# Transformer block with routed experts on one NeuronCore: attention keys and queries in two parts of 11 bits instead of three parts of 8, and one score product for two heads instead of two

## The chip, the cores and the metric

The kernel runs on one core of one Trainium2 chip. The core has a matrix engine (TensorE, PE in the profile; its weight loads are PEld), VectorE (DVE), ScalarE (ACT) and GpSimd (POOL), and SyncE (SP) that issues most DMAs. Each engine runs its own instructions in order; they meet through semaphores. The metric is the device time of one execution in microseconds.

## What is computed

Input z is (4, 1024, 256) in float32. The part that this change touches is the attention of 16 heads of 16 dimensions:

```python
x = L0_attn_z
zn = layernorm(layernorm(x)) * ln_scale + ln_bias
q, k, v = split(zn @ w_qkv)            # 16 heads of 16
scores = einsum('bhqd,bhkd->bhqk', q, k) / 4
att = softmax(scores)                  # over 1024 keys
out = einsum('bhal,bhlv->bhav', att, v) @ w_proj + b_proj
x = x + layernorm(layernorm(x) + out)
# then a gated feed-forward with 8 routed experts (top 1) for every second token,
# x = x + layernorm(ffn(layernorm(x)))
```

## The kernel before

The four batches run through one pipeline of **slots**. A batch has 64 slots: 4 groups of 4 heads, two halves of 512 queries, 8 tiles of 128 keys (`SL = 64`, 256 slots for all). Slot t does the **max products** of slot t and the **scores** of the slot 12 earlier (`LEAD = 12`).

*Scores.* A float32 score is made of 16-bit products. A key or query is split in three bfloat16 parts of 8 bits; `PRODUCTS` lists six pairs of parts that are kept. The six times 16 dimensions do not fit in the 64 rows that one head has of the 128, so they stand in two planes: plane 0 has the pairs of the largest parts (48 rows), plane 1 the other three and two rows with the negated maximum (50 rows). `kp` and `qp` hold them, stacked by DMAs (`STACK`, `pack_step`, L377 to L396). Two heads, one in rows 0 to 63 and one in rows 64 to 127, run at the same time. `scores(a)` (a = 0 and 1, two heads each) issues four matmuls of 512 columns: two planes, two heads (L1047). ScalarE takes the exp of the 1024 columns (L870) and `value_product` multiplies them with the values in float32 (L1061).

*Maxima.* The softmax needs each query's largest score before. It is taken from plane 0 alone: four max products a slot (L1028), each into one bank of the PSUM **ring** of three banks, each reduced by VectorE (L1324). Every 8 slots the maxima are transposed ("mt"), split in two parts (`mp`, L1332 and L1334) and sent by DMA into the last two rows of `qp`.

*The ring* also takes all other results: transposes of normalized inputs ("z", "x", "u"), projections of keys and queries ("qk"), values ("v"), the output ("p") and the feed-forward ("h", "w"). `ring_order` writes by hand in which slot each stands (`Z_AT`, `QK_AT` and so on); in a slot they come before max0. Bank i is free again when the engine that takes the item three places earlier is done.

*On TensorE* a slot has: ring items of other kinds, max products 0 and 1, `scores(0)`, `scores(1)`, max products 2 and 3, and the value products of the slot before.

*The parts.* ScalarE copies a projection to `qkf` (L805) and its first part to `parts` (L807). Then three passes over 1024 columns: the residual (`residual`, L1314 on VectorE or L640 on GpSimd), the second part as its cast (L646, or L1377 at the start) and the third part (L649, L1379). For the next batch's first keys VectorE makes the residual in slot 35 and GpSimd the other two.

Of the kernel before, what the change touches and what calls it, by code (L numbers as in the profile page):

```python
# [14 lines left out]
GH = 4  # L15
# [6 lines left out]
KM = KR + 2  # L22
# [6 lines left out]
PRODUCTS = [(0, 0), (1, 0), (0, 1), (2, 0), (1, 1), (0, 2)]  # L29
STACK = [(par, r // 3 * 4, 64 * par + r % 3 * HD, k, q) for r, (k, q) in enumerate(PRODUCTS) for par in range(2)]  # L30
# [103 lines left out]
def plane_of(h, plane):  # L134

    return h // 8 * 8 + 4 * plane + h % 8 // 2


def build(nc, x, ln_params, w_q, w_k, w_v, w_proj, b_proj, index_b, index_t, sw12, sb12, sw3, sb3,
          hidden_ln, gate_w, gate_b, exp_bias, ew12, ebias12, ew3, eb3, out):  # L140
    f32, bf16, i32, u32 = mybir.dt.float32, mybir.dt.bfloat16, mybir.dt.int32, mybir.dt.uint32
# [9 lines left out]
    with ExitStack() as ctx:  # L151
# [19 lines left out]
        parts = sb("parts", [P, 2, 3, N], bf16)  # L171
        qp = sb("qp", [P, NH, H, HALF], bf16)
        kp = sb("kp", [P, H, N], bf16)
# [25 lines left out]
        mp = sb("mp", [GH * QT, 2, 2, P], bf16)  # L199
# [42 lines left out]
        fixed = resid[0:2, 0:HALF].bitcast(bf16)  # L242
# [38 lines left out]
        s_resid = sem("residual_of_first_part")  # L281
        s_second = sem("second_part")
        s_third = sem("third_part")
# [78 lines left out]
        LARGEST = [item for item in STACK if item[1] == 0]  # L362
        REST = [item for item in STACK if item[1] > 0]
# [11 lines left out]
        def _(sp):  # L375
# [3 lines left out]
            def pack_step(b, c, i):  # L379


                for n in range(3 * i, 3 * i + 3):
                    if n in (0, len(STACK)):
                        sp.wait_ge(s_third, 2 * KD * b + c + (n > 0) + 1)
                        if b > 0:
                            sp.wait_ge(s_av, SL * (b - 1) + (SL // 2 if c < 2 else SL))
                    par, plane, row, k, q = STACK[n if n < len(STACK) else (n - len(STACK)) // NH]
                    rows, h0, src = slice(row, row + HD), c // 2 * 8 + plane, slice(par * 64, par * 64 + 64)
# [42 lines left out]
            for par in range(2):  # L431
                for h in (0, 8):
                    first = plane_of(h, 1)
                    sp.dma_start(kp[64 * par + KR:64 * par + KM, first:first + 4, :],
# [6 lines left out]
            for part in range(2):  # L441
                if part == 1:
                    sp.wait_ge(s_second, 1)
                for par, plane, row, k, q in LARGEST:
                    if k == part:
                        sp.dma_start(kp[row:row + HD, plane:plane + 4, :], parts[par * 64:par * 64 + 64, 0, k, :])\
                          .then_inc(s_k0, 16)
            sp.wait_ge(s_part, 4)
            for part in range(2):
                if part == 1:  # L450
                    sp.wait_ge(s_second, 2)
                for par, plane, row, k, q in LARGEST:
                    if par == 1 and q == part:
                        sp.dma_start(qp[row:row + HD, 0, plane:plane + 4, :],
# [1192 lines left out]
```

## Time and profile before

| what | value |
|---|---|
| median of 3 runs | 995.28 us (992.9 to 995.99) |
| profiled execution | 993.8 us, its span 992.0 us |
| TensorE busy | 927.3 us (93%) |
| VectorE busy | 798.6 us (81%) |
| ScalarE busy | 617.0 us (62%) |
| GpSimd busy | 352.1 us (35%) |
| score products, L1047, 2048 of them | 275.2 us |
| max products, L1028, 1024 | 246.4 us |
| value products, L1061, 2048 instructions | 273.6 us |

Times of rows are microseconds from the start of the span. In a timeline a row is: start, length, engine, line, operation, out<-in, shapes, how many were merged, and in brackets the idle time before it with what ended it. The rows of the windows view have: from and to, its length, busy time and number of instructions of PE, PEld, DVE, ACT and POOL, then the granted clock of TensorE as a share of its full speed, the DMA share and GB/s. "L1028 <- DVE mx L1324" in a wait says that VectorE's instruction of line 1324 ended it. A float32 matmul is two instructions. A matmul's row lasts from its start until its last column is written, and the next one starts before that.

### The profile page before, as it was taken

What the parts mean: (1) busy time and instruction counts of PE and PEld (TensorE: products, weight loads), DVE (VectorE), ACT (ScalarE), POOL (GpSimd) and SP (SyncE); (2) the same over time, 40 slices, a digit from 0 to 9 for tenths busy, and PEclk for the clock granted to TensorE, in tenths of its full rate; (3) what the DMA queues carried; (4) which work ended last, traced back from release to release, by engine and by line L of the source; (5) the groups of instructions that cost most, each with busy time, mean ns of one, the idle gap of its engine ahead of it and who ended that gap; (6) DMA issues with size and microseconds to landing.
All of it is one profiled execution on the core that took longest, in us unless ns stands there. A gap on an engine that the chain in (4) does not pass through costs nothing.

```text
span 992.0 us, 16504 instructions
## 1 busy us (share of the span) xinstructions
PE 927.3 (93%) x6202; PEld 373.5 (38%) x6204; DVE 798.6 (81%) x1568; ACT 617.0 (62%) x720; POOL 352.1 (35%) x473
## 2 busy tenths in 40 slices
PE   5879999999999999999999999999999989957985
PEld 3323332323343344333343343332422423136763
DVE  4688879898979878889889979889799798265765
ACT  3116778777867777777767767777676777801110
POOL 3052003004635253229733623258243232822113
PEclk9778999999999999999999999999999999988998
DMA  4924120620260305300631033104430000240001
GB/s 135 155 32 64 47 55 12 98 61 8 75 109 24 97 13 77 75 13 22 113 110 60 8 54 80 36 8 104 91 99 13 12 13 20 95 170 22 1 0 64
DMA packets 60544, 58.14 MB, mean 59 GB/s; under 512 B 19136, under 2 KB 49680, under 8 KB 60080
## 3 DMA queue, kind: packets, MB, share of 16 engines
q1 hardware_dynamic: 59840, 55.83, 25.6%
q8 instruction: 49, 0.80, 0.4%
q0 software_dynamic: 384, 1.05, 0.3%
q10 hardware_dynamic: 240, 0.20, 0.2%
q14 instruction: 31, 0.25, 0.1%
HBM read 18.06 MB, written 9.17 MB: 27 GB/s over the span
## 4 chain that ended last, share of the span: by engine, by line
PE 79%; DVE 9%; ACT 3%; issue 3%; DMA 2%; POOL 2%; SPq 1%; ACTq 0%; POOLq 0%; DVEq 0%
PE obank L1061 22%; PE sc L1047 19%; PE ring L1028 16%; PE ring L946 9%; PE ring L953 4%; DVE mx L1324 4%; PE sc L1178 3%; PE ring L938 2%; DVE st L1253 2%; ACT prob L870 1%; PE sc L953 1%; DMA x_sb<-x 1%; DMA qp<-parts 1%; PE ring L1071 1%; ACT zT L773 0%
## 5 line engine op out<-in xcount | busy, mean ns | idle before, releaser
L1324 DVE TENSOR_REDUCE mx<-ring 128x1 f32<-128x512 f32 x1024 | 634.6, 681 | 107.9 <-PE ring L1028 106.9
L870 ACT ACTIVATE prob<-sc 128x1024 f32<-128x1024 f32 x512 | 495.8, 1021 | 132.6 <-PE sc L1047 131.4
L1047 PE MATMUL sc<-qp,kp 48*128 48x512 bf16 (+1 forms) x2048 | 275.2, 380 | 2.2 <-DMA qp<-mp 0.9
L1061 PE MATMUL obank<-prob,vaug 128*32 128x512 f32 x2048 | 273.6, 606 | 0.7 <-ACT prob L870 0.7
L1028 PE MATMUL ring<-kp,qp 48*128 48x512 bf16 x1024 | 246.4, 392 | 17.0 <-DVE mx L1324 13.0
L1028 PEld LDWEIGHTS ring<-kp,qp 48*128 48x128 bf16 x1024 | 75.0, 93 | 296.4 <-DVE mx L1324 228.5
L1047 PEld LDWEIGHTS sc<-qp,kp 48*128 48x128 bf16 (+1 forms) x2048 | 98.9, 95 | 106.8 <-ACT prob L870 25.2
L626 POOL TENSOR_TENSOR hid<-hid,b 128x512 f32<-128x512 f32 x24 | 30.3, 1271 | 110.9 <-ACT hid L831 110.9
L1061 PEld LDWEIGHTS obank<-prob,vaug 128*32 128x32 f32 x2048 | 40.3, 108 | 66.1 <-issue 63.9
L640 POOL TENSOR_TENSOR resid<-qkf,parts 128x1024 f32<-128x1024 f32 x11 | 23.4, 2131 | 114.4 <-ACT parts L807 114.4
L634 POOL TENSOR_TENSOR yA<-yA,sums 128x512 f32<-128x512 f32 x15 | 19.0, 1269 | 110.4 <-DMA sums<-reciprocal_scratch 110.4
L646 POOL TENSOR_SCALAR parts<-resid 128x1024 bf16<-128x1024 f32 x14 | 14.7, 1050 | 106.7 <-DVE resid L1314 105.7
L946 PE MATMUL ring<-w,yT 128*128 128x256 f32 x192 | 47.6, 400 | 1.4 <-ACT yT L773 1.4
L946 PEld LDWEIGHTS ring<-w,yT 128*128 128x128 f32 x192 | 36.7, 198 | 16.8 <-DVE mx L1324 5.0
L938 PE MATMUL ring<-ident,zn 128*128 128x128 f32 x128 | 19.4, 303 | 23.9 <-DVE zn L1351 12.1
L805 ACT ACTIVATE qkf<-ring 128x512 f32<-128x512 f32 x28 | 16.7, 595 | 30.5 <-PE ring L953 29.1
L572 POOL TENSOR_TENSOR sum_m<-st 128x8 f32<-128x8 f32 x15 | 3.1, 209 | 79.6 <-DVE st L1253 79.6
L649 POOL TENSOR_TENSOR parts<-resid,parts 128x1024 bf16<-128x1024 f32 x14 | 29.8, 2131 | 1.2
L773 ACT ACTIVATE yT<-ring 128x512 f32<-128x512 f32 x16 | 8.8, 595 | 33.2 <-PE ring L938 33.2
L1178 PE MATMUL sc<-kp,qp 128*128 128x256 f32 x128 | 29.1, 381 | 0.1
L946 PE MATMUL ring<-wv,zT 128*128 128x256 f32 x128 | 28.8, 379 | 0.0
L938 PEld LDWEIGHTS ring<-ident,zn 128*128 128x128 f32 x128 | 16.4, 157 | 28.6 <-issue 12.9
(212 smaller groups left out, 797.9 us busy)
## 6 DMA issues: line engine op xcount, KB each, us to landing
kp<-parts SPq DMA_DIRECT2D x96, 128.0 KB, 4.9
qp<-parts SPq DMA_DIRECT2D x189, 64.0 KB, 2.9
x_sb<-x SPq DMA_DIRECT2D x7, 1024.0 KB, 6.1
out<-hid SPq DMA_DIRECT2D x4, 1024.0 KB, 5.3
yA<-oT SPq DMA_DIRECT2D x124, 32.0 KB
sums<-reciprocal_scratch SPq DMA_DIRECT2D x31, 128.0 KB
x_scratch<-x SPq DMA_DIRECT2D x3, 1024.0 KB, 4.5
qp<-mp SPq DMA_DIRECT2D x128, 2.0 KB
```

Source lines behind the costliest of these rows:

```text
L626: nc.gpsimd.tensor_tensor(hid[:, t, :], hid[:, t, :], {"h": b12, "w": b3}[kind][:, :] .rearrange("p (o d) -> p o d", o=1).to_broadcast([P, ...
L640: nc.gpsimd.tensor_tensor(resid[:, :], qkf[:, :], parts[:, c % 2, 0, :], ALU.subtract)\
L649: nc.gpsimd.tensor_tensor(parts[:, c % 2, 2, :], resid[:, :], parts[:, c % 2, 1, :], ALU.subtract).then_inc(s_third, 1)
L870: nc.scalar.activation(prob[:, e % 2, 2 * a:2 * a + 2, :].rearrange("p g n -> p (g n)"), sbuf2[a][:, :], ACT.Exp, scale=0.25).then_inc(s_f ...
L938: ins = nc.tensor.transpose(dst[:, t * P:(t + 1) * P], src[:, 4 * h + t, kk * P:(kk + 1) * P], ident[:, :])
L946: ins = nc.tensor.matmul(dst[:, (t - 2 * i) * D:(t - 2 * i + 1) * D], src[:, k, t * P:(t + 1) * P], w[:, k, :], start=(k == 0), stop=(k == ...
L953: ins = nc.tensor.matmul(dst[:, :], w[:, k, mt * P:(mt + 1) * P], zT[:, k, h * HALF:(h + 1) * HALF], start=(k == 0), stop=(k == KD - 1))
L1028: nc.tensor.matmul(dst[:, :], qp[rows, qh, h, qt * P:(qt + 1) * P], kp[rows, h, kh * HALF:(kh + 1) * HALF], start=True, stop=True).then_in ...
L1047: ins = nc.tensor.matmul(dst[:, j * HALF:(j + 1) * HALF], kp[rows, h, kt * P:(kt + 1) * P], qp[rows, qh, h, :], start=plane == 0, stop=pla ...
L1061: ins = nc.tensor.matmul(obank[i * VW:(i + 1) * VW, :], vaug[:, b % 2, kt, c0:c0 + VW], prob[:, v % 2, i, :], start=(kt == 0), stop=(kt == ...
L1178: ins = nc.tensor.matmul(expert_bank(i)[:, t, :], lhs[:, m], w, start=False, stop=stop, skip_group_check=True)
L1324: nc.vector.tensor_reduce(mx[:, u % 2, n:n + 1], src[:, :], AX.X, ALU.max).then_inc(rv_free, 1)
```

## The change

Keys and queries are scaled by a power of two each, so that they fit in float16, and split in two float16 parts of 11 bits. Four pairs of parts are kept, the smallest of them in 14 of the 16 dimensions: 3 x 16 + 14 + 2 rows for the maximum are the 64 rows of a head. So one matmul makes a head's scores. The max products are the same first 48 rows.

```diff
-KM = KR + 2
+KS = HD - 2
+KM = KR + KS + 2
-PRODUCTS = [(0, 0), (1, 0), (0, 1), (2, 0), (1, 1), (0, 2)]
+PRODUCTS = [(0, 0), (1, 0), (0, 1), (1, 1)]
...
-                    for plane in range(2):
-                        h = plane_of(g * GH + 2 * a, plane)
-                        for j in range(2):
-                            rows = slice(64 * j, 64 * j + (KM if plane else KR))
-                            ins = nc.tensor.matmul(dst[:, j * HALF:(j + 1) * HALF], kp[rows, h, kt * P:(kt + 1) * P],
-                                                   qp[rows, qh, h, :], start=plane == 0, stop=plane == 1)
+                    h = g * GH // 2 + a
+                    for j in range(2):
+                        rows = slice(64 * j, 64 * j + KM)
+                        ins = nc.tensor.matmul(dst[:, j * HALF:(j + 1) * HALF], kp[rows, h, kt * P:(kt + 1) * P],
+                                               qp[rows, qh, h, :], start=True, stop=True)
```

A part now takes one pass in place of three, on VectorE for the first two parts of the kernel and on GpSimd for all others; the one of slot 35 moves from VectorE to GpSimd, slot 34:

```diff
-            def split(b, c):
-                n = 2 * KD * b + c
-                pool.wait_ge(s_resid, n + 1)
-                nc.gpsimd.tensor_scalar(parts[:, c % 2, 1, :], resid[:, :], 1.0, 0.0, ALU.mult, ALU.add)\
                     .then_inc(s_second, 1)
-                pool.wait_ge(s_second, n + 1)
-                nc.gpsimd.tensor_tensor(parts[:, c % 2, 2, :], resid[:, :], parts[:, c % 2, 1, :],
-                                        ALU.subtract).then_inc(s_third, 1)
...
-                if w + 1 < B and tau == 35:
-                    split(w + 1, 0)
+                if w + 1 < B and tau == 34:
+                    second_part(w + 1, 0)
```

The scales come from a bound made at the start: the weights times the layer norm's scale and bias are squared on ScalarE, summed over their rows by a matmul with ones, the largest taken on VectorE, its root on GpSimd, and a power of two of it on VectorE. ScalarE applies the scale as it evacuates a projection, and the exp takes it out again; both scales are operands in memory, one per partition:

```diff
+            for a, w in enumerate((wk, wq)):
+                for k in range(KD):
+                    for r in range(2):
+                        nc.scalar.activation(wsq[:, a, k, r, :], w[:, k, :], ACT.Square, scale=lnp[:, r, k:k + 1])\
+                            .then_inc(s_wsq, 1)
...
-                    nc.scalar.activation(qkf[:, half], src[:, :], ACT.Copy).then_inc(taken, 1)
+                    nc.scalar.activation(qkf[:, half], src[:, :], ACT.Identity, scale=scale[:, c % 2:c % 2 + 1]).then_inc(taken, 1)
...
-                                             sbuf2[a][:, :], ACT.Exp, scale=0.25).then_inc(s_free, 1)
+                                             sbuf2[a][:, :], ACT.Exp, scale=unscale[:, 0:1]).then_inc(s_free, 1)
...
-                for n in range(3 * i, 3 * i + 3):
+                for n in range(2 * i, 2 * i + 2):
...
-                    nc.vector.tensor_copy(mp[:, u % 2, 0, :], src[0:GH * QT, 0:P]).then_inc(s_m1, 1)
+                    nc.vector.tensor_scalar(mp[:, u % 2, 0, :], src[0:GH * QT, 0:P], 1.0 / MAX_ROW, None, ALU.mult)\
+                        .then_inc(s_m1, 1)
...
-                    nc.vector.tensor_tensor(mp[:, u % 2, 1, :], src[0:GH * QT, 0:P], mp[:, u % 2, 0, :],
-                                            ALU.subtract).then_inc(rv_free, 1)
-
-            nc.vector.memset(fixed[:, :], 1.0).then_inc(s_src, 1)
+                    nc.vector.scalar_tensor_tensor(mp[:, u % 2, 1, :], src[0:GH * QT, 0:P], 1.0 / MAX_ROW,
+                                                   mp[:, u % 2, 0, :], ALU.mult, ALU.subtract).then_inc(rv_free, 1)
```

TensorE's instructions of a slot, before. `ring0` to `ring2` are the ring's banks, `sc0` and `sc1` the two score banks; L1071 is the maxima's transpose, so this is a slot with one of them:

```order
L1071 MATMUL ring0<-ident,nm 16x128 [waits negated_maxima,ring_taken_by_vector]
L1028 MATMUL ring1<-kp,qp 128x512 [waits ring_taken_by_vector]
L1028 MATMUL ring2<-kp,qp 128x512 [waits ring_taken_by_vector]
L1047 MATMUL sc0<-qp,kp 128x512 [waits score_buffer_taken]
L1047 MATMUL sc0<-qp,kp 128x512 x3
L1047 MATMUL sc1<-qp,kp 128x512 [waits score_buffer_taken]
L1047 MATMUL sc1<-qp,kp 128x512 x3
L1028 MATMUL ring0<-kp,qp 128x512 [waits ring_taken_by_vector]
L1028 MATMUL ring1<-kp,qp 128x512 [waits ring_taken_by_vector]
L1061 MATMUL obank<-prob,vaug 32x512 [waits score_buffer_taken]
L1061 MATMUL obank<-prob,vaug 32x512 x3
```

The same slot with the change:

```order
L1080 MATMUL ring0<-ident,nm 16x128 [waits negated_maxima,ring_taken_by_vector]
L1038 MATMUL ring1<-kp,qp 128x512 [waits ring_taken_by_vector]
L1038 MATMUL ring2<-kp,qp 128x512 [waits ring_taken_by_vector]
L1056 MATMUL sc0<-qp,kp 128x512 [waits score_buffer_taken]
L1056 MATMUL sc0<-qp,kp 128x512
L1056 MATMUL sc1<-qp,kp 128x512 [waits score_buffer_taken]
L1056 MATMUL sc1<-qp,kp 128x512
L1038 MATMUL ring0<-kp,qp 128x512 [waits ring_taken_by_vector]
L1038 MATMUL ring1<-kp,qp 128x512 [waits ring_taken_by_vector]
L1070 MATMUL obank<-prob,vaug 32x512 [waits score_buffer_taken]
L1070 MATMUL obank<-prob,vaug 32x512 x3
```

Four score products are gone; nothing else moved, and the fourth max product still goes to the bank of the first, `ring1`.

ScalarE's first instructions, before (`zT` is the transposed input, `lnp` the layer norm's scale and bias):

```order
L839 ACT_TABLE_LOAD
L839 ACTIVATE ex<-mhalf 128x2 [waits exponents_made]
L773 ACTIVATE zT<-ring,lnp 128x512 [waits ring_filled,attention_weights_loaded]
L773 ACTIVATE zT<-ring,lnp 128x512 [waits ring_filled] x3
L805 ACTIVATE qkf<-ring 128x512 [waits ring_filled]
L807 ACTIVATE parts<-qkf 128x512 [waits ring_taken_by_scalar]
```

And with the change (`hid` and `act` are buffers that are free at the start):

```order
L835 ACT_TABLE_LOAD
L835 ACTIVATE ex<-mhalf 128x2 [waits exponents_made]
L840 ACTIVATE hid<-wk,lnp 128x256 [waits attention_weights_loaded]
L840 ACTIVATE hid<-wk,lnp 128x256 x3
L840 ACTIVATE hid<-wq,lnp 128x256 x4
L768 ACTIVATE zT<-ring,lnp 128x512 [waits ring_filled] x4
L801 ACTIVATE qkf<-ring,scale 128x512 [waits scales_of_keys_and_queries,ring_filled]
L803 ACTIVATE parts<-qkf 128x512 [waits ring_taken_by_scalar]
```

Eight squares stand before the first evacuation, and TensorE has eight small matmuls that wait for them before its first transpose.

## Rows read from the trace of the kernel before

**Rows 1.** The page's chain that ended last, by line.
```profile
PE obank L1061 22%; PE sc L1047 19%; PE ring L1028 16%; PE ring L946 9%; PE ring L953 4%; DVE mx L1324 4%; PE sc L1178 3%; PE ring L938 2%; DVE st L1253 2%; ACT prob L870 1%; PE sc L953 1%; DMA x_sb<-x 1%; DMA qp<-parts 1%; PE ring L1071 1%; ACT zT L773 0%
```
**Rows 2.** Busy time by windows: first slots with scores, and a stretch of the middle.
```profile
72.60:84.20 11.60, 11.24 (x53) 3.32 (x52) 8.33 (x14) 5.45 (x6) 8.21 (x14) 0.57 0.95 108
...
100.00:300.00 200.00, 199.48 (x1452) 69.68 (x1451) 174.49 (x311) 150.04 (x171) 48.00 (x51) 1.00 0.28 58
```
**Rows 3.** Waits from 100 to 840 us: total, times, longest.
```profile
PEld ring L1028 <- DVE mx L1324: 197.3, 384, 3.2
```
**Rows 4.** Timeline of TensorE in one plain slot, 262.13 to 264.62.
```profile
262.13 0.39 PE L1028 MATMUL ring<-kp,qp 48*128 48x512 bf16 x2
...
262.36 1.03 PE L1047 MATMUL sc<-qp,kp 48*128 48x512 bf16 x8
...
263.23 0.46 PE L1028 MATMUL ring<-kp,qp 48*128 48x512 bf16 x2
263.30 0.09 PEld L1028 LDWEIGHTS ring<-kp,qp 48*128 48x128 bf16 x1 [0.19 <-DVE mx L1324]
...
263.62 1.06 PE L1061 MATMUL obank<-prob,vaug 128*32 128x512 f32 x8
...
264.62 0.39 PE L1028 MATMUL ring<-kp,qp 48*128 48x512 bf16 x2
```
**Rows 5.** Timeline of a slot after two transposes of z.
```profile
256.41 1.45 ACT L773 ACTIVATE zT<-ring,lnp 128x512 f32<-128x512 f32 x2 [0.55 <-PE ring L938]
...
256.68 0.39 PE L1028 MATMUL ring<-kp,qp 48*128 48x512 bf16 x1
...
257.24 0.39 PE L1028 MATMUL ring<-kp,qp 48*128 48x512 bf16 x1 [0.17 <-ACT zT L773]
...
258.65 1.07 PE L1061 MATMUL obank<-prob,vaug 128*32 128x512 f32 x8
```
**Rows 6.** Timeline of a slot after two transposes of x, TensorE.
```profile
358.87 0.70 PE L1028 MATMUL ring<-kp,qp 48*128 48x512 bf16 x2
...
360.59 1.06 PE L1061 MATMUL obank<-prob,vaug 128*32 128x512 f32 x8
```
**Rows 7.** Timeline of the slot after the next batch's second projection, TensorE.
```profile
345.09 0.60 PE L1047 MATMUL sc<-qp,kp 48*128 48x512 bf16 x4
...
345.96 0.61 PE L1047 MATMUL sc<-qp,kp 48*128 48x512 bf16 x4 [0.27 <-ACT prob L870]
```
**Rows 8.** Timelines of the last twelve slots, without max products: ScalarE and TensorE.
```profile
852.11 1.05 PE L1047 MATMUL sc<-qp,kp 48*128 48x512 bf16 x8 [0.91 <-DMA qp<-mp]
...
862.26 1.02 ACT L870 ACTIVATE prob<-sc 128x1024 f32<-128x1024 f32 x1
...
863.61 3.91 ACT L870 ACTIVATE prob<-sc 128x1024 f32<-128x1024 f32 x4 [0.33 <-PE sc L1047]
867.85 1.94 ACT L870 ACTIVATE prob<-sc 128x1024 f32<-128x1024 f32 x2 [0.33 <-PE sc L1047]
```
**Rows 9.** ScalarE's groups by shape: count, busy us, mean ns of one, idle.
```profile
L773 ACT ACTIVATE zT<-ring,lnp 128x512 f32<-128x512 f32 x16 | 11.8, 774 | 14.0 <-PE ring L938 13.8
...
L773 ACT ACTIVATE yT<-ring 128x512 f32<-128x512 f32 x16 | 8.8, 595 | 33.2 <-PE ring L938 33.2
...
L909 ACT ACTIVATE zT<-ring,hln 128x256 f32<-128x256 f32 x2 | 1.1, 562 | 1.7 <-PE ring L1199 1.7
...
L904 ACT ACTIVATE zn<-sc 128x256 f32<-128x256 f32 x2 | 0.8, 383 | 16.2 <-PE sc L1178 16.2
```
**Rows 10.** Timeline of the start.
```profile
3.29 0.47 SPq L429 DMA_DIRECT2D wv<-w_v  x1
...
12.13 3.65 PE L938 MATMUL ring<-ident,zn 128*128 128x128 f32 x16 [12.13 <-DVE zn L1351]
...
22.92 0.69 DVE L1377 CAST parts<-resid 128x1024 bf16<-128x1024 f32 x1
```
**Rows 11.** DMA issues of the first 40 us: KB each, us to landing.
```profile
wv<-w_v SPq DMA_DIRECT2D x1, 256.0 KB, 5.3
```

More of the change, by code:

```diff
@@ L25 @@
 MT = M // P
-PRODUCTS = [(0, 0), (1, 0), (0, 1), (2, 0), (1, 1), (0, 2)]
-STACK = [(par, r // 3 * 4, 64 * par + r % 3 * HD, k, q) for r, (k, q) in enumerate(PRODUCTS) for par in range(2)]
+PRODUCTS = [(0, 0), (1, 0), (0, 1), (1, 1)]
+STACK = [(par, HD if r < 3 else KS, 64 * par + r * HD, k, q) for r, (k, q) in enumerate(PRODUCTS) for par in range(2)]
+TOP = 2.0 ** 13
+MAX_ROW = 2.0 ** 15
 ONES = struct.unpack("<f", struct.pack("<HH", 0x3F80, 0x3F80))[0]
@@ L198, in build @@
         nm = sb("nm", [P, 2, GH * QT])
-        mp = sb("mp", [GH * QT, 2, 2, P], bf16)
+        mp = sb("mp", [GH * QT, 2, 2, P], f16)
+        wmax, wroot, power, scale, unscale = (sb(n, [P, 2]) for n in ("wmax", "wroot", "power", "scale", "unscale"))
         st6 = [sb(f"st6{i}", [P, NT, 6]) for i in range(2)]
@@ L663, in _ @@
             rstd_of("z", 0, 0, NT, 0)
+            pool.wait_ge(s_wmax, 1)
+            step(nc.gpsimd.tensor_scalar(wroot[:, :], wmax[:, :], 2.0 * D, 1e-30, ALU.mult, ALU.add))
+            nc.gpsimd.tensor_tensor(wroot[:, :], wroot[:, :], mhalf[:, 0:2], ALU.pow).then_inc(s_wroot, 1)
             pool.wait_ge(s_rstd["z"], 1)
@@ L670, in _ @@
                 if tau == (4 if w == 0 else 3) and w < B:
-                    residual(w, 2)
-                    split(w, 2)
+                    second_part(w, 2)
                 if tau == (11 if w == 0 else 4) and w + 1 < B:
@@ L675, in _ @@
                 if tau == (6 if w == 0 else 5) and w < B:
-                    residual(w, 3)
-                    split(w, 3)
+                    second_part(w, 3)
                 if w == B - 1 and tau == 5:
@@ L713, in _ @@
                 if w + 1 < B and tau == 40:
-                    residual(w + 1, 1)
-                    split(w + 1, 1)
+                    second_part(w + 1, 1)
                 if 1 <= w < B:
@@ L866, in _ @@
                     if 0 <= e < NS:
+                        if e == 0 and a == 0:
+                            sc.wait_ge(s_power, 4)
                         if e >= 2 and a == 0:
@@ L1003, in _ @@
             pe.wait_ge(s_first, C_FIRST)
+            pe.wait_ge(s_ones, 1)
+            for a in range(2):
+                for i in range(2 * KD):
+                    pe.wait_ge(s_wsq, 2 * KD * a + i + 1)
+                    ins = nc.tensor.matmul(sbuf2[0][:, a * D:(a + 1) * D], ones, wsq[:, a, i // 2, i % 2, :], start=(i == 0),
+                                           stop=(i == 2 * KD - 1))
+                ins.then_inc(s_bound, 1)
             for key in RING_AT[-1]:
@@ L1355, in _ @@
             ins.then_inc(s_norm["z"], 1)
+            ve.wait_ge(s_bound, 2)
+            nc.vector.tensor_reduce(wmax[:, :], sbuf2[0][:, 0:2 * D].rearrange("p (a d) -> p a d", a=2), AX.X, ALU.max)\
+                .then_inc(s_wmax, 1)
             ve.wait_ge(s_idxin, 32)
@@ L1423, in _ @@
                     nc.vector.tensor_tensor(half, half, sums[0:GH * HD, 1, :], ALU.mult).then_inc(s_div64, 1)
-                if w + 1 < B and tau == 35:
-                    residual(w + 1, 0)
                 if 1 <= w < B and tau in (47, 49):
```

113 lines of the change are left out of this document (59 added, 54 removed).

## Prediction

> **What bounds the kernel now.** The page first. Its chain puts 19% of the span on the score products (L1047) [rows 1], and in the middle of the kernel TensorE shows matmuls for 199.48 of 200 us, VectorE 174.49 [rows 2]. Read so far, the score products are the thing to halve. But each matmul's row lasts longer than the step to the next one, so short waits lie hidden under it. The list of waits shows them: weight loads of the max products (L1028) waited 197.3 us for VectorE's reductions between 100 and 840 us, 384 times [rows 3].
>
> So one plain slot has to be read instruction by instruction [rows 4]. Its four max products go to the three ring banks; call them max0 to max3. Max3 gets the bank that max0 had, and so waits until VectorE has reduced max0. In the slot that starts at 262.13:
> - max0 and max1 at 262.13, eight score products from 262.36, max2 at 263.23;
> - the weights of max3 at 263.30, after a wait that VectorE ended: 1.17 after max0;
> - the value products at 263.62 (0.32 later), the next max0 at 264.62 (1.00 later).
>
> 1.17 + 0.32 + 1.00 is the slot's 2.49 us, and this loop (max0, its reduction, max3, value products, next max0) does not contain the score products. They fill time that TensorE would wait through, with 0.07 us to spare (263.23 against 263.30). Projections and transposes stand between the value products and the next max0, so their time adds to the loop and is paid in full before and after the change. By my count of the slots from 12 to 255, nine in ten have this form.
>
> A rule of the Trainium skill fits what this row shows (Trainium Kernel Development and Optimization, Performance Expectations): matmul busy time is a bad measure of distance to the roofline, because matmuls are pipelined. The chain's share, read as time to be won, would give 100 us or more; rows 4 give nothing in such a slot.
>
> **The change part by part.** The sum is made against the profiled execution, 993.8 us, which is 1.5 under the median of 995.28.
>
> *Four score products in place of eight, plain slots.* Two pairs go, 0.44 us of the 0.87 between 262.36 and 263.23. Max2 is issued 0.44 earlier, max3 still at +1.17. Gain 0 [rows 4].
>
> *Slots in which max3 is late for another reason.* Where a transposed z or u is evacuated, max1 waits for ScalarE and pushes the score products back, and max3 comes after them [rows 5]: max1 goes at 257.24, the value products at 258.65. With four score products TensorE is through them by 257.9; max2 needs the second evacuation (256.41 + 1.45 = 257.86), max3 the reduction of max0 (256.68 + 1.17 = 257.85). The value products come at about 258.24: 0.41 won. There are six z slots and three of u alike: 3.7 us. In the six x slots the value products start 1.72 after max0 instead of 1.49 [rows 6]: 0.23 each, 1.4 us. In batches 1 and 2 one slot has its second half of scores 0.87 after the first instead of 0.44, waiting for an exp [rows 7]; the exp is late because ScalarE waited for VectorE's residual, which GpSimd, idle there, now makes a slot earlier. 0.43 less the spare 0.07 is 0.35, twice: 0.7 us. Eight slots with a shortfall of 0.03 add 0.2. Together 6.0 (5.0 to 6.2, the lower end if the exp stays late).
>
> *The first slots with scores.* The granted clock is 0.57 there [rows 2], mostly the lower level, and TensorE, not VectorE, sets the pace. The two pairs cost 0.86 at that level: 0.86 in two slots and about half in the third, 2.2 in all. But if the clock comes back at the same time as before, the work that arrives 1.7 us sooner finds it low for longer, and some 1.0 is given back. I take 1.2, bounds 0 and 2.2.
>
> *The twelve slots after the last max product.* Only scores, exps and value products run. Two slots take 4.24 us (863.61 to 867.85), of which ScalarE works 3.91 and waits 0.33 for scores [rows 8]. With short score products ScalarE is the bound. Its exps get a scale from memory. The price of that is bounded by evacuations: with scale and bias from memory 774 ns against 595 at 512 columns, 562 against 383 at 256, so 179 for both together whatever the length [rows 9]. I take half, 0.09, for the scale alone; bounds 0 and 0.18. Two exps back to back take 1.94 and one alone 1.02 [rows 8], so 0.92 from start to start; four take 4 x 1.01 = 4.04, 0.10 won a slot. Two of the slots end in a wait of 0.91 for the maxima's rows [rows 8] that swallows it: ten slots, 1.0 us (at 0.18: 4.40, a loss of 0.8).
>
> The Trainium skill (ScalarE: Activation LUTs, What ACT_TABLE_LOAD costs) gives about 93 ns for each pointer operand, so it splits the pair's 179 ns evenly. By it the sum is the same; with all 179 on the scale it is the rival below.
>
> *Exps in the other slots.* 0.09 on two exps is met by scores that are ready 0.22 sooner, and two exps fit in 2.49 with 0.5 to spare. 0.
>
> *The start.* New before the first transposes: eight squares on ScalarE and eight small matmuls. The last weights were issued at 3.29 and took 5.3, so they are there at 8.6 to 9.1 [rows 10, 11]. A 128x256 evacuation takes 383 [rows 9]; with one pointer and an overlap of 0.1, some 0.38 a square, 3.0 us: done at 11.7 to 12.2. The small matmuls follow each square, so the transposes start at 12.0 to 12.5 instead of 12.13 [rows 10]: 0.2 lost (0 to 0.4). The root and the powers of two run on GpSimd and VectorE while TensorE transposes and projects. Against that, a part's 0.69 us cast [rows 10] leaves the way between the second query part and its DMA, on which the first max product waits. ScalarE's two pointer evacuations there take 0.2 of it back. Net 0.3 won (0.4 lost to 0.7 won).
>
> *Hidden, at 0.* A residual on VectorE (three times, under the projection of keys and queries); two of three GpSimd passes for each part; a third of the stacking DMAs and their issues on SP (no TensorE wait for them stands in the middle); two small ops in the maxima's split, of the same size as those replaced. A slot with its transpose that ran longer by 0.1 would cost 3 us over 32.
>
> *Sum.* 6.0 + 1.2 + 1.0 + 0.3 = 8.5. 993.8 - 8.5 = 985.3; at the median's level 995.28 - 8.5 = **986.8 us**. Bounds of the terms: 3.8 to 10.1, so 985.2 to 991.5; with the 1.5 us by which runs of the kernel before scatter, 983.5 to 993.
>
> **The rivals.**
> *The score products are on the path*, as the chain says [rows 1]. Then 244 slots win 0.44 each: 107 us, 888. Against it: max3's wait is ended by VectorE [rows 3, 4].
>
> *The clock falls in the middle (slower).* TensorE will wait longer in each plain slot. It had the lower level for most of 72.6 to 84.2, a stretch in which it waited, and 1.00 between 100 and 300 [rows 2], with 0.19 of waiting in a plain slot [rows 4]. At the lower level the value products take 2.0 instead of 1.0, so a slot is at least 3.5. A low stretch of 11.6 us, as that one, then holds 3.3 slots instead of 4.7 and costs 3.4. From three such stretches on nothing is won; if half of the middle were low it would cost 100. At six of them, 8.5 - 6 x 3.4 = -11.9, it is 1,007.
> The Trainium skill has the rule behind it (TensorE: Matmul & The Clock Gate, Part 1): the clock is gated by how busy the engine has been, and low is the resting state. No row shows a plain slot with half its score products.
>
> *The start gives it back.* With other work at the start the low stretch that ends near 84 us [rows 2] lasts longer, or another one is added: one or two times 3.4 us, 990 to 994.
>
> *The scale pointer costs 0.18 an exp.* The last slots lose 0.8 instead of winning 1.0, and in some 14 slots after keys and queries the exps run late by up to 0.2: 8.5 - 1.8 - 2.5 = 4.2, 991.1.
>
> *It does not do what it says.* The order has half the score instructions, so only their rate can fail: no row has the 16-bit float type of the change. The nearest is the other 16-bit type, 0.22 a pair [rows 4], and I take that. At twice that time two more pairs stand in the loop of each slot, 0.44 x 244: 1,095 us.
>
> **How the numbers follow.** Forecast 0.64; scores on the path 0.03; clock in the middle 0.08; start gives it back 0.12, nearly half of it under 992.3; scale pointer 0.10; 16-bit rate 0.03. The band of 0.3%, about what a measurement of this kernel can tell, is 992.3 to 998.3. Faster: 0.64 + 0.03 + 0.10 + 0.05 = 0.82; same 0.08; slower 0.10, the clock, the rate and little else. The range 981 to 993.5 takes in the forecast, the scale pointer and the better half of the start.
>
> **What would show it.** In the profile after: plain slots still 2.49 from max0 to max0, the wait of max3's weights grown from 0.19 to about 0.6 and ended by VectorE; TensorE's busy time down by tens of microseconds with the span down by under ten; z slots with value products 1.56 after max0, x slots 1.49; exps at 1.11 instead of 1.02; the last slots at 2.0; the first transposes by 12.5. I am wrong if plain slots get shorter, if the clock between 100 and 840 us is under 1.00, or if exps grow by 0.18.

## The result and the profile after

| | before | after |
|---|---|---|
| median | 994.89 us (4 runs, 992.9 to 995.99) | 984.22 us (4 runs, 983.47 to 986.59) |
| profiled execution, its span | 993.8, 992.0 us | 983.9, 982.1 us |
| TensorE busy | 927.3 us | 882.3 us |
| ScalarE busy | 617.0 us | 663.7 us |
| score products | 275.2 us, 2048 of them | 167.9 us, 1024 of them |

The ratio after to before is 0.9899, 95% interval 0.9876 to 0.9923: 10.7 us by the medians, 9.9 by the two profiled executions. The forecast was 986.8, within 981 to 993.5.

The groups of the page (line, engine, operation, out<-in, shapes, count | busy us, mean ns | idle before and what ended it) and the wait that answers to [rows 3]:

```profile
L873 ACT ACTIVATE prob<-sc,unscale 128x1024 f32<-128x1024 f32 x512 | 539.1, 1113 | 85.2 <-PE sc L1056 83.9
L1038 PEld LDWEIGHTS ring<-kp,qp 48*128 48x128 f16 x1024 | 74.1, 93 | 361.4 <-DVE mx L1331 301.3
L1056 PE MATMUL sc<-qp,kp 64*128 64x512 f16 x1024 | 167.9, 381 | 14.0 <-ACT prob L873 13.3
L801 ACT ACTIVATE qkf<-ring,scale 128x512 f32<-128x512 f32 x28 | 19.2, 686 | 27.1 <-PE ring L956 25.7
```
```profile
PEld ring L1038 <- DVE mx L1331: 267.1, 393, 3.4
```

The rows of the score products lost 107 us, TensorE as a whole 45 (rows of matmuls overlap, and those of the max products are drawn longer now: 299.4 us for 246.4). The max products' weights wait 70 us more for VectorE (197.3 to 267.1, between 100 and 840 us before, 90 and 830 after). So most of the time saved became waiting.

The plain slot of [rows 4] is now this one:

```profile
262.73 0.39 PE L1038 MATMUL ring<-kp,qp 48*128 48x512 f16 x2
...
262.95 0.60 PE L1056 MATMUL sc<-qp,kp 64*128 64x512 f16 x4
...
263.39 0.90 PE L1038 MATMUL ring<-kp,qp 48*128 48x512 f16 x2
...
263.89 0.09 PEld L1038 LDWEIGHTS ring<-kp,qp 48*128 48x128 f16 x1 [0.60 <-DVE mx L1331]
...
264.21 1.06 PE L1070 MATMUL obank<-prob,vaug 128*32 128x512 f32 x8
...
265.21 0.39 PE L1038 MATMUL ring<-kp,qp 48*128 48x512 f16 x2
```

Max2 comes 0.66 us after max0 instead of 1.10, and still max3's weights come after 1.16 and the next max0 after 2.48. The wait grew from 0.19 to 0.60.

**Where the time went**, slot by slot (start of max0 to start of the next, both traces; gains positive):

| stretch | gain, us |
|---|---|
| until slot 12 begins (72.7 to 69.2) | 3.5 |
| slots 12 to 14, the first with scores | 2.4 |
| six z and three u slots, 0.42 each | 3.7 |
| six x slots, 0.23 each | 1.4 |
| slots 100 and 164, behind keys and queries, 0.28 each | 0.6 |
| slots 79, 143, 207 and 212 | 1.9 |
| ten slots with 0.05 more each | -0.5 |
| slots 218, 241 and 242, at the lower clock | -3.6 |
| the last twelve slots | 1.3 |
| behind them | -0.7 |

These add up to 10.0, for 9.9 measured. A z slot and an x slot of after, beside [rows 5, 6]:

```profile
250.23 0.39 PE L1038 MATMUL ring<-kp,qp 48*128 48x512 f16 x1
...
251.78 1.07 PE L1070 MATMUL obank<-prob,vaug 128*32 128x512 f32 x8
252.78 0.39 PE L1038 MATMUL ring<-kp,qp 48*128 48x512 f16 x2
```
```profile
354.46 0.71 PE L1038 MATMUL ring<-kp,qp 48*128 48x512 f16 x2
...
355.95 1.07 PE L1070 MATMUL obank<-prob,vaug 128*32 128x512 f32 x8
```

The value products start 1.55 (z) and 1.49 us (x) after max0; the prediction had 1.56 and 1.49. The stretches at the lower clock, as windows (times, length, busy of PE, PEld, DVE, ACT, POOL, granted clock, DMA share, GB/s), and the wait ahead of the second:

```profile
714.10:717.50 3.40, 3.40 (x16) 0.60 (x13) 3.04 (x6) 2.12 (x2) 3.21 (x5) 0.50 0.05 5
789.20:796.00 6.80, 6.50 (x27) 1.17 (x29) 4.61 (x8) 2.12 (x2) 6.26 (x17) 0.50 0.06 22
```
```profile
789.50 0.60 PE L1038 MATMUL ring<-kp,qp 48*128 48x512 f16 x1 [3.08 <-DVE mx L1331]
```

Between 100 and 300 us the clock is 1.00 as before.

The stretch at the lower clock into which the first slots with scores fall, before, after, and in the experiment "Score products alone" below:

```profile
62.10:82.60 20.50, 17.11 (x54) 4.37 (x55) 17.52 (x35) 3.88 (x4) 13.84 (x26) 0.50 0.68 87
```
```profile
58.70:75.80 17.10, 14.06 (x37) 2.69 (x37) 16.49 (x33) 4.24 (x4) 8.63 (x21) 0.50 0.50 68
```
```profile
59.20:79.60 20.40, 17.22 (x55) 4.39 (x57) 17.42 (x34) 4.45 (x5) 10.45 (x24) 0.50 0.42 57
```

### The profile page after: what moved, and what is told of

Read it like the earlier page. It is cut to its first block and busy times, and to the rows that moved or that the text cites. A ratio compares the mean times of both kernels' runs of the same rounds, so it can differ in the third digit from the quotient of the medians.

```text
span 982.1 us, 14337 instructions
## 1 busy us (share of the span) xinstructions
PE 882.3 (90%) x5188; PEld 319.8 (33%) x5188; DVE 792.7 (81%) x1568; ACT 663.7 (68%) x728; POOL 314.5 (32%) x450
## 3 DMA queue, kind: packets, MB, share of 16 engines
q0 software_dynamic: 384, 1.05, 0.3%
## 5 line engine op out<-in xcount | busy, mean ns | idle before, releaser
L873 ACT ACTIVATE prob<-sc,unscale 128x1024 f32<-128x1024 f32 x512 | 539.1, 1113 | 85.2 <-PE sc L1056 83.9
L1038 PE MATMUL ring<-kp,qp 48*128 48x512 f16 x1024 | 299.4, 395 | 43.5 <-DVE mx L1331 22.5
L1038 PEld LDWEIGHTS ring<-kp,qp 48*128 48x128 f16 x1024 | 74.1, 93 | 361.4 <-DVE mx L1331 301.3
L1056 PE MATMUL sc<-qp,kp 64*128 64x512 f16 x1024 | 167.9, 381 | 14.0 <-ACT prob L873 13.3
L644 POOL TENSOR_TENSOR parts<-qkf,parts 128x1024 f16<-128x1024 f32 x14 | 29.9, 2134 | 209.6 <-ACT parts L803 209.6
L1056 PEld LDWEIGHTS sc<-qp,kp 64*128 64x128 f16 x1024 | 50.4, 95 | 92.3 <-ACT prob L873 83.9
L801 ACT ACTIVATE qkf<-ring,scale 128x512 f32<-128x512 f32 x28 | 19.2, 686 | 27.1 <-PE ring L956 25.7
L827 ACT ACTIVATE hid<-ring 128x512 f32<-128x512 f32 x24 | 14.3, 597 | 20.4 <-PE ring L949 20.4
L956 PE MATMUL ring<-zT,wq 128*128 128x512 f32 x56 | 25.8, 603 | 0.0
L1187 PEld LDWEIGHTS sc<-kp,qp 128*128 128x128 f32 x128 | 24.2, 190 | 4.4 <-DVE qp L1536 0.3
```

Of the source, the lines that this page charges most:

```text
L644: nc.gpsimd.tensor_tensor(parts[:, c % 2, 1, :], qkf[:, :], parts[:, c % 2, 0, :], ALU.subtract)\
L801: nc.scalar.activation(qkf[:, half], src[:, :], ACT.Identity, scale=scale[:, c % 2:c % 2 + 1]).then_inc(taken, 1)
L873: nc.scalar.activation(prob[:, e % 2, 2 * a:2 * a + 2, :].rearrange("p g n -> p (g n)"), sbuf2[a][:, :], ACT.Exp, scale=unscale[:, 0:1]).t ...
L956: ins = nc.tensor.matmul(dst[:, :], w[:, k, mt * P:(mt + 1) * P], zT[:, k, h * HALF:(h + 1) * HALF], start=(k == 0), stop=(k == KD - 1))
L1038: nc.tensor.matmul(dst[:, :], qp[rows, qh, h, qt * P:(qt + 1) * P], kp[rows, h, kh * HALF:(kh + 1) * HALF], start=True, stop=True).then_in ...
L1056: ins = nc.tensor.matmul(dst[:, j * HALF:(j + 1) * HALF], kp[rows, h, kt * P:(kt + 1) * P], qp[rows, qh, h, :], start=True, stop=True)
```

## Experiments

### Score products alone

Every score product of the changed kernel is issued twice into the same bank:

```diff
+                    for j in range(2):
+                        rows = slice(64 * j, 64 * j + KM)
+                        nc.tensor.matmul(dst[...], kp[...], qp[...], start=True, stop=True)
                     for j in range(2):
                         rows = slice(64 * j, 64 * j + KM)
                         ins = nc.tensor.matmul(dst[...], kp[...], qp[...], start=True, stop=True)
```

> The changed kernel with each of its four score products of a slot issued twice into the same bank, so that TensorE has eight of them again and all else is as changed. Loop theory (max0, its reduction, max3, value products set a plain slot, score products fill a wait): plain slots stay at 2.49 us; what comes back is the z, u and x slots (about 5.2 us by the two traces), the first cold slots with scores (2.4), the slot after keys and queries (0.6) and the last twelve slots (0.7), in all 8.9, less up to 3.7 if the two stretches of low clock at 714 and 789 us go away because TensorE has more to do: 5 to 9 us over the changed kernel, 989 to 993. Rival, score products on the path: 0.44 in each of 244 slots, 107 us more, about 1,091.

Measured: 994.53 us (10 runs), ratio to the kernel before 1.000 (0.9983 to 1.0016). A plain slot of it on TensorE:

```profile
260.30 0.39 PE L1038 MATMUL ring<-kp,qp 48*128 48x512 f16 x2
260.52 0.38 PE L1056 MATMUL sc<-qp,kp 64*128 64x512 f16 x2
...
261.39 0.47 PE L1038 MATMUL ring<-kp,qp 48*128 48x512 f16 x2
261.47 0.09 PEld L1038 LDWEIGHTS ring<-kp,qp 48*128 48x128 f16 x1 [0.20 <-DVE mx L1335]
...
261.79 1.06 PE L1074 MATMUL obank<-prob,vaug 128*32 128x512 f32 x8
262.78 0.39 PE L1038 MATMUL ring<-kp,qp 48*128 48x512 f16 x2
```

Eight products again, four pairs of 0.22: the wait shrinks to 0.20 and the slot stays (max3's weights 1.17 after max0, value products 1.49, next max0 2.48). The rival (1,091) is out. What came back is in the slots named: 0.41 in each z and u slot, 0.23 in each x slot, 2.5 in slots 12 to 14, 1.8 in the last twelve. A further 0.22 came in twelve slots next to keys and queries, ten of which the kernel before runs without it: doubled scores and the longer exps together make an exp late there. So the gain goes when the score products are doubled, and the other parts of the change sum to nothing within the interval (1.7 us). That sum has large terms in this one trace: against the kernel before, 3.2 won until slot 12 and 1.9 in slots 79, 143, 207 and 212, and lost 2.7 in twelve slots next to keys and queries, 1.6 in the slots 240 to 242 with a stretch at the lower clock, 0.5 in the last twelve slots and 0.3 behind them.

### The price of the pointers

```diff
-nc.scalar.activation(prob[...], sbuf2[a][:, :], ACT.Exp, scale=unscale[:, 0:1])
+nc.scalar.activation(prob[...], sbuf2[a][:, :], ACT.Exp, scale=0.25 / 2.0 ** 20)
-nc.scalar.activation(qkf[:, half], src[:, :], ACT.Identity, scale=scale[:, c % 2:c % 2 + 1])
+nc.scalar.activation(qkf[:, half], src[:, :], ACT.Copy, scale=2.0 ** 10)
```

> The changed kernel with fixed numbers for the three scales (2 to the 10th for keys and queries, the matching one in the exp) in place of operands in memory; the bound and the powers of two are still worked out, and nobody reads them. Theory: the pointer costs 0.09 us an exp; it shows in the last twelve slots (about 1.0 us) and in some 14 slots after keys and queries, where an exp is late (0.05 each, 0.7 in all): 1.5 to 2 us under the changed kernel, 982 to 983, and exps at 1.02 instead of 1.11. Rival: exps are covered everywhere, no change, 984.2.

Measured: 981.94 us (981.53 to 982.96), 2.3 less than the change by medians of different calls (the ratios to the kernel before, 0.9878 and 0.9899, have intervals that overlap, so the rows have to settle it). The exps of the last slots in the timelines of the changed kernel and of this one, each followed by two of them in a narrower window, and this one's group of exps:

```profile
845.07 14.18 ACT L873 ACTIVATE prob<-sc,unscale 128x1024 f32<-128x1024 f32 x14
...
849.06 2.15 ACT L873 ACTIVATE prob<-sc,unscale 128x1024 f32<-128x1024 f32 x2
```
```profile
842.92 13.37 ACT L873 ACTIVATE prob<-sc 128x1024 f32<-128x1024 f32 x14
...
848.58 1.94 ACT L873 ACTIVATE prob<-sc 128x1024 f32<-128x1024 f32 x2
```
```profile
L873 ACT ACTIVATE prob<-sc 128x1024 f32<-128x1024 f32 x512 | 495.5, 1021 | 113.3 <-PE sc L1056 111.7
```

An exp takes 1113 against 1021 ns on average, so the pointer costs 92; the Trainium skill (ScalarE: Activation LUTs, What ACT_TABLE_LOAD costs) has about 93, and the trace agrees. The mean steps of the two rows of 14, (14.18 - 1.11) / 13 = 1.005 and (13.37 - 1.02) / 13 = 0.950, seem to say that in a row it costs only 0.055. They do not: with the short exps three of the thirteen steps (those to 846.75, 850.55 and 854.35) are 1.05 to 1.12 long, because ScalarE stops there for scores, and the other ten are 0.90 to 0.92, as the 1.94 of two exps less 1.02 shows. Against steps of 1.00 with the pointer it costs 0.09 in a row too; TensorE takes part of what shorter exps would win. Between the two profiled executions (2.1 us) the last twelve slots gave 1.2, twelve slots next to keys and queries 0.07 or 0.08 each (0.9), and other places of the lower clock 1.5 in the middle; 0.6 until slot 15 and 0.9 behind the last exp were lost. This version fits only inputs whose bound allows the fixed numbers.

### The bound, and the start

The version with immediate scales, with squares, small matmuls, roots and powers of two left out too, so the bound is not computed.

> The same with fixed scales, and with the bound left out: no squares, no small matmuls with the matrix of ones, no roots and powers of two. Theory: the eight small matmuls before the first transposes start TensorE's work 3 us sooner, so that its clock rises sooner (14.4 instead of 17.7 us in the two traces), and this gave 1.3 us until the first max product and more in the slots behind it; without them this is lost: 1.5 to 3 us slower than with fixed scales alone, first max reduction near 33.8 us instead of 32.5. Rival: the bound costs time at the start (squares ahead of the evacuations, 0.2) and the earlier start comes from the shorter way of the second part: no change or up to 0.5 faster.

Measured: 981.98 us (981.5 to 985.51) against 981.94; first max reduction at 32.44 us. My theory (the small matmuls bring the clock up) falls: the wk projection still ran at full rate, its eight instructions in 3.60 us against 4.69 before. What then made the start 3.5 us shorter? The fourteen traces of this study begin as the kernel before (four) or as the changed one (ten; the two with immediate scales leave part of that start out, and the one with more stacking DMAs adds to it), and the clock rises at other times:

| start | clock up at, us | first max reduction | first reduction of slot 12 |
|---|---|---|---|
| of before | 17.7 (two traces) | 33.8 | 73.7 |
| of before | 16.2, 16.7 (two) | 33.1 | 71.4 |
| of after | 14.4 to 15.3 (six) | 32.4 to 32.7 | 70.2 to 70.8 |
| of after | 16.0 to 16.1 (three) | 32.9 to 33.2 | 71.2 to 71.4 |
| of after | 17.1 (one) | 33.6 | 72.0 |

The windows from 46 to 52 us (columns as above) of the kernel before, of the changed one, and of the experiment "the kernel before in halves" below, whose start is that of before:

```profile
46.00:52.00 6.00, 5.64 (x10) 1.40 (x8) 2.48 (x4) 1.23 (x2) 0.00 (x0) 0.51 0.63 173
```
```profile
46.00:52.00 6.00, 4.86 (x14) 1.65 (x13) 4.87 (x8) 2.27 (x4) 1.49 (x1) 1.00 0.00 0
```
```profile
46.00:52.00 6.00, 5.07 (x14) 1.40 (x14) 3.97 (x7) 2.46 (x4) 0.29 (x1) 0.88 0.51 156
```

Where the clock rose at like times, 16.0 to 16.2 us, the two starts are within 0.2 us of each other at slot 12 (71.4 against 71.2 to 71.4). That is one trace of the kernel before's start against three of the other. By it the 3.5 us are mostly not work saved but the time at which the clock rose. Whether the change makes an early rise likelier, these traces are too few to say.

### The number of stacking DMAs

The smallest pair of parts is sent three times, twice into planes that nobody reads, with three DMAs a step instead of two:

```diff
+STACK += [(par, KS - 1, row - d, k, q) for d in (0, HD) for par, dims, row, k, q in STACK if dims == KS]
-                for n in range(2 * i, 2 * i + 2):
+                for n in range(3 * i, 3 * i + 3):
```

> The changed kernel with as many stacking DMAs as before: the last pair of parts is sent three times, twice of them into planes that nobody reads, three issues a step on the SyncE queue instead of two. Theory: the gains of 0.40, 0.18 and 0.45 us in the slots 79, 143 and 207 and of 0.82 in slot 212, where before a reduction or a projection waited for a DMA queued behind the stacking DMAs, come from the shorter queue; they come back, 1.5 to 2 us, and the start may lose up to 1 more: 985.5 to 987.5. Rival: those gains come from other shifts (an earlier exp, another place of the DMA against the slot), and the number of stacking DMAs costs nothing: 984 to 984.5.

Measured: 985.81 us (984.14 to 987.23). The medians alone, 1.6 apart over overlapping runs, would not settle it; the slots do. The wait in the kernel before, and in this version:

```profile
272.81 0.25 DVE L1307 RECIPROCAL over<-total 128x16 f32<-128x16 f32 x1 [0.31 <-DMA total<-oT]
```
```profile
267.44 0.25 DVE L1317 RECIPROCAL over<-total 128x16 f32<-128x16 f32 x1 [0.37 <-DMA total<-oT]
```

VectorE again waits for the DMA of the sums that stands behind the stacking DMAs on SP's queue; slots 78, 142 and 206 (by the first reduction of a slot; by max0 they are 79, 143 and 207) lost 0.47, 0.14 and 0.49, against 0.41, 0.19 and 0.45 won by the change, and slots 84 and 148 lost 0.3 each. Slot 212 (0.82 won) did not come back, so its cause stays open.

### Opening the loop

If the loop sets the slot, another order should shorten it. Five orders were tried, each with a reason and a number, and none gained. First, max3 behind the value products:

```diff
                 if t < NS:
-                    max_products(range(2, 4))
+                    max_products(range(2, 3))
                 if 0 <= e - 1 < NS:
                     value_product(e - 1)
+                if t < NS:
+                    max_products(range(3, 4))
```

> The changed kernel with the fourth max product of a slot issued behind the value products instead of ahead of them. This opens the loop: max3 no longer holds back the value products, and VectorE's four reductions (4 x 0.598 = 2.39 us) or TensorE's own work (4 x 0.24 + 2 x 0.22 + 1.00 = 2.40) set the slot. Loop theory: plain slots fall from 2.49 to 2.40 or 2.42, some 200 slots x 0.07 to 0.09 = 14 to 18 us, and the slots with transposes or projections, whose time now lies beside the reductions, up to 0.4 more each (30 slots, 5 to 10 us): 960 to 970. Rival, that something else sets 2.49 (the reductions themselves with their gaps, or the exps): no change, 984.

Measured: 994.75 us (992.99 to 996.29), where I had 960 to 970. A plain slot:

```profile
263.03 0.10 PEld L1038 LDWEIGHTS ring<-kp,qp 48*128 48x128 f16 x2 [0.84 <-DVE mx L1333]
...
264.20 0.09 PEld L1038 LDWEIGHTS ring<-kp,qp 48*128 48x128 f16 x1 [0.20 <-DVE mx L1333]
264.21 0.39 PE L1038 MATMUL ring<-kp,qp 48*128 48x512 f16 x1
...
264.52 1.07 PE L1070 MATMUL obank<-prob,vaug 128*32 128x512 f32 x8
...
265.52 0.10 PEld L1038 LDWEIGHTS ring<-kp,qp 48*128 48x128 f16 x2 [0.84 <-DVE mx L1333]
```

263.03 to 265.52 is 2.49 again. I had taken for an opened loop what was the same loop, turned: with three banks and four products a slot, the last product ahead of the value products has the bank of the first one behind them, wherever they stand. The slots with transposes or projections lost 0.2 to 0.6 each, 10 us in all.

The same in the kernel before:

> The kernel before with the same move of the fourth max product behind the value products. With eight score products TensorE needs 4 x 0.24 + 4 x 0.22 + 1.00 = 2.84 us a slot if rows 4 add up like that, or 2.49 less the wait of 0.07 = 2.42 if the products follow each other as closely as in that slot. Loop theory: TensorE is the bound as soon as the loop is open, so the gain is at most the spare of 0.07 x 200 = 14 us and less than that of the same move in the changed kernel by at least 10 us; I expect 985 to 995. Rival: the move alone gives 20 us or more here too, and the halved score products have nothing to do with it: 970 to 975.

Measured: 1,023.87 us, ratio 1.029, where I had 985 to 995. Plain slots in a row came to 2.57 or 2.59:

```profile
277.75 0.77 PE L1028 MATMUL ring<-kp,qp 48*128 48x512 bf16 x3
278.13 1.25 PE L1047 MATMUL sc<-qp,kp 48*128 48x512 bf16 x8
...
279.01 0.38 PE L1028 MATMUL ring<-kp,qp 48*128 48x512 bf16 x1
...
279.32 1.07 PE L1061 MATMUL obank<-prob,vaug 128*32 128x512 f32 x8
```

Between the products that share a bank (max3 at 277.75, max2 at 279.01) now stand two more max products and the eight score products: 1.26, over the 1.17 that the reduction takes. So here the score products do count. Slots between two with projections lost more: of the hundred slots from 21 on that take 2.49 in the changed kernel, 28 take 3.01 here.

Next, the value products in two halves of 256 queries with max3 between:

> The changed kernel with the value products of a slot in two halves of 256 queries, the fourth max product between them. Moving max3 behind all value products only turned the loop (max3, its reduction, max2 of the next slot, value products, max3: again 1.17 + 0.31 + 1.00), since with three banks and four products a slot the last product ahead of the value products always has the bank of the first one behind them. With a block of half the length the loop is 2.0 and no longer the bound. Theory: VectorE's reductions (4 x 0.598 = 2.39) set a plain slot, provided TensorE needs less (about 2.3); 0.09 x 190 slots = 17 us, less what a second set of weight loads and late slots cost: 962 to 975. Rival: TensorE's extra fills make its own work as long as the loop was: no change or slower, 984 to 1,000.

Measured: 992.52 us (988.78 to 995.38), ratio 0.998, where I had 962 to 975. Plain slots fell to 2.43 or 2.45, where TensorE's own work sets them. But the slots with z, u, keys and queries and the first ones with scores lost more (0.3 to 1.9 each).

> The kernel before with the same two halves of the value products. With eight score products TensorE's own work in a slot is 0.44 us longer, about 2.7 against the loop's 2.49. Theory: as soon as the loop is open TensorE is the bound, and it is slower than the kernel before by some 200 x 0.2 = 40 us: 1,020 to 1,040; so what the change bought is room on TensorE, which this order turns into time and the old one does not. Rival: it gains as much as the changed kernel does from the halves: 975 to 985.

Measured: 1,082.21 us, ratio 1.086, plain slots at 2.86. The direction was right, the size (1,020 to 1,040) was not: I had counted 200 slots at 2.7 and TensorE needs 2.86, and this trace has 41 us at the lower clock behind 873 us.

Then a new order in which TensorE needs least, with products in pairs and half of the scores a slot early:

```diff
                 if t < NS:
                     max_products(range(0, 2))
-                    scores(0)
-                    scores(1)
+                    scores(1, e)
+                    value_product(e - 1, 0)
                     max_products(range(2, 4))
-                    value_product(e - 1)
+                    scores(0, e + 1)
+                    value_product(e - 1, 1)
```

> The changed kernel with a slot in another order on TensorE, from slot 18 on: max0 and max1, the second score pair, the first half (256 queries) of the value products, max2 and max3, the first score pair of the next slot, the second half of the value products. In the order with halves alone a plain slot came to 2.45, and TensorE set it: 0.23 + 0.44 + 0.30 + 0.57 + 0.31 + 0.57 = 2.42, since max2 and max3 stand apart there and pay 0.3 each. Paired they cost 0.3 together, so TensorE needs about 2.15. Theory: VectorE's 4 x 0.598 = 2.39 sets the plain slot, 0.09 x 180 = 16 us, and slots in which scores, maxima or values came late win too; the weight loads of the second half cost nothing where VectorE is the bound: 963 to 975. Rival: exps and value products now wait for each other, or the low clock around slot 241 takes more; no gain, 982 to 992.

Measured: 996.87 us (995.51 to 1,001.67), ratio 1.004, where I had 963 to 975. In the plain slots the theory held:

```profile
262.44 0.48 PE L1039 MATMUL ring<-kp,qp 48*128 48x512 f16 x2
...
263.63 0.48 PE L1039 MATMUL ring<-kp,qp 48*128 48x512 f16 x2
...
264.83 0.48 PE L1039 MATMUL ring<-kp,qp 48*128 48x512 f16 x2
...
545.79 0.39 PE L1057 MATMUL sc<-qp,kp 64*128 64x512 f16 x2 [0.95 <-ACT prob L874]
```

262.44 to 264.83 is 2.39, four reductions of 0.598 without a gap. But VectorE has other work (a reciprocal, the maxima's transposes, statistics) in many slots. In the old order that work uses the 0.09 that VectorE waits in each slot; here it adds, and such slots come to 2.55 or more. And where an exp is late, half the scores stand in its way: the last row is a slot with keys and queries, 0.91 longer than before, twelve times. Both score pairs together gave no more:

> As the new slot order, but both score pairs stay together behind max0 and max1. By the rows at hand max2 then starts 0.23 + 0.44 + 0.57 = 1.24 us after max0 where VectorE wants its result by 1.17 + 0.43, so VectorE waits some 0.05 a slot: 2.43 to 2.45 a plain slot, 0.05 x 180 = 9 us: 972 to 980. Rival: as with halves alone, no gain, 985 to 992.

Measured: 993.91 us, ratio 1.001, where I had 972 to 980; of those hundred slots 40 still take 2.49 and 31 take 2.53.

Last, the new order only in the 185 slots without transposes and projections:

> The changed kernel with the new slot order only in the 185 slots from 21 on that hold no transposes or projections; all others keep the old order. Taken slot by slot from the traces of the changed kernel and of the new order everywhere: the 48 plain slots at 2.49 fall to 2.39 or 2.40 (4.6 us), the slot ahead of a projection gives 0.2 to 0.3 (some 30 slots, 5 to 7 us), the slots in which VectorE has other work stay at 2.55, and the losses of the slots with keys and queries (12 x 0.91), z and u (0.4 each) and others are avoided: 12 us in all by the sum over these slots, of which 2.3 is the low clock at slots 218 and 241: 972, between 967 and 979. Rival: what was lost in the other slots comes with the switch between the orders, no gain over the changed kernel, 984 or more.

Measured: 998.29 us, 14 over the changed kernel, where 12 were to be won. The rival was right. Behind a slot in the old order the first half of the value products comes 0.97 us after max0 instead of 1.49 while the exps have not moved, and the score pair of the next slot (258.92) waits 0.24 for one:

```profile
257.04 0.39 PE L1039 MATMUL ring<-kp,qp 48*128 48x512 f16 x2
...
258.01 0.64 PE L1077 MATMUL obank<-prob,vaug 128*32 128x256 f32 x8
...
258.92 0.10 PEld L1057 LDWEIGHTS sc<-qp,kp 64*128 64x128 f16 x2 [0.24 <-ACT prob L874]
...
259.81 0.39 PE L1039 MATMUL ring<-kp,qp 48*128 48x512 f16 x2
```

From 257.04 to 259.81 is 2.77 instead of 2.49, and so behind most switches. Adding up slots from two traces had assumed that each slot stands alone.

> The kernel before with the same new order in the same slots. With eight score products TensorE needs two pairs more, about 2.15 + 0.44 = 2.59 a slot, over the 2.49 of the old order. Theory: what the change bought is room on TensorE, so here the new order turns to a loss of 0.07 to 0.1 in the plain slots and about 0.05 in those at 2.55, less what the slots ahead of a projection give: 995 to 1,010. Rival: the new order alone wins, whatever the score products: 980 to 985.

Measured: 1,040.44 us, ratio 1.047. Its plain slots:

```profile
270.05 0.39 PE L1029 MATMUL ring<-kp,qp 48*128 48x512 bf16 x2
...
272.72 0.39 PE L1029 MATMUL ring<-kp,qp 48*128 48x512 bf16 x2
```

2.67, where the same order with four score products had 2.39. So the saved products are worth 0.28 us a slot in an order in which TensorE sets the pace, and nothing in the order the kernel has. I had 2.59 and 995 to 1,010.

## Why the prediction came out right

- **The loop** is shown: plain slots at 2.49 with four products, with eight, and with the loop turned; 2.39 when halves open it. The views that pointed the other way (chain, busy share) would have given 888.
- **Slots with a late max3**: 6.0 predicted, 5.2 measured (3.7 + 1.4 + 0.6 - 0.5). z, u and x were right to 0.01. The slots behind keys and queries gave 0.28 of 0.35, and ten slots lost 0.05 where I had 0.03 won for eight: the exps, longer by 0.09, are late there, which I had put down as hidden. Immediate scales gave those twelve slots 0.07 or 0.08 back.
- **First slots with scores**: 1.2 predicted, 2.4 measured, above my bound of 2.2. The step that failed is the 1.0 given back through the clock. I had the clock come back when it did before; it came back 6.8 us sooner, with the slots only 3.5 us ahead. The stretch at the lower clock took 17.1 us instead of 20.5, and 20.4 again with the doubled products. So the three slots won 0.85, 1.06 and 0.44, the third at 2.49, its time at the full clock. Why the stretch is shorter no run shows; the orders with values in halves and with the new slot order had 23.9 with four products.
- **Last twelve slots**: 1.0 predicted, 1.3 measured; ScalarE is the bound, as said, with steps of 1.00 for the 1.01 that I took; the price of 0.09 for the pointer was right.
- **The start**: 0.3 predicted, 3.5 in the trace. The steps themselves were near (first transposes at 12.10, as before; the starts equal within 0.2 at like clock times). What I had not counted is what the time at which the clock rises is worth by slot 12: 2.3 us between the starts of the kernel before (71.4 to 73.7), 1.7 between those of the changed one (70.24 to 71.96).
- **Hidden at nothing**: wrong in one place. I had looked for waits of TensorE for the stacking DMAs; the wait was VectorE's reciprocal, behind them on SP, and gave 1.1, with 0.8 in slot 212 whose cause is open.
- **The clock in the middle**, a rival at 0.08, came in small: 3.6 us lost behind two long waits of TensorE for VectorE. The waits at these two places were 1.13 and 2.70 us before, where the clock stayed at 1.00, and are 1.51 and 3.08 now. It is not settled that the halved products bring it: every trace with them has such stretches late in the kernel, but so has the one with doubled products (3.4 us at 800) and two of the four of the kernel before and its variants (6.8 and 41 us). The prediction called 72.6 to 84.2 a stretch in which TensorE waited; its row has matmuls for 11.24 of 11.60 us and so does not show that.

So 986.8 was near 984.2 partly by balance: 1.9 in slots 79, 143, 207 and 212, 1.2 in the first slots with scores, 3.2 at the start and 0.3 in the last twelve, all over what was foreseen, stand against 3.6 at the lower clock, 0.8 in late slots and 0.7 behind the last slots, whose cause is open. The loop was right; that the other terms cancelled to 1.4 us between the profiled executions was luck.

## What to carry to other kernels

Follow one repeated stretch instruction by instruction and find the loop that closes on itself; work that is not in it fills a wait, and halving it wins only where that loop is broken by something else. Count banks against products before moving one: an order that looks new can be the same loop turned. Before a gain at the start of a kernel is put down to a change, compare when the clock rose.

## What the hardware showed

- A reduction of VectorE in a row starts 0.598 us after the one ahead, while its own row lasts 0.681; the first after a wait starts 0.68 later. One such gap a slot (0.68, 0.61, 0.60 and 0.60 in a plain slot of the changed kernel) is the whole difference between 2.39 and 2.49.
- The float32 value products take 1.00 us for 512 queries and 0.57 for 256, so halves cost 0.14 a slot.
- In seven traces with the same instructions up to the first max product the clock rose between 14.4 and 17.1 us, and the slots at 70 us moved by 1.7.
- In the kernel's own slot order the stretch at the lower clock into which the first slots with scores fall took 17.1 us with four score products and 20.5 with eight; why is open.
